# Attentional factorization machine on one core: 31 product columns per batch row in place of 32, products of both batch groups made at once

## What is computed

```python
F, B, K, H, VOCAB = 32, 2048, 64, 64, 12500      # sizes of this case
V = emb_v[x]                                      # F x B x K, gathered rows
iu, ju = np.triu_indices(F, k=1)
VV = V[iu] * V[ju]                                # 496 pairs of different fields
hid = relu(einsum('pbk,kh->pbh', VV, at_w) + at_b)
score = einsum('pbh,ho->pbo', hid, at_h)
pooled = sum(VV * score, axis=0)
logit = pooled @ p + w0 + sum(w1[x], axis=0)
y = sigmoid(logit)                                # B x 1
```

## Time and profile before

| | |
|---|---|
| runs | 842.78, 843.54 and 846.02 us, median 843.54 |
| span of the profiled execution | 835.8 us |
| median of the runs less that span | 7.7 us |
| mean TensorE clock granted | 0.992 of full |
| PE, DVE, ACT, POOL busy | 94%, 86%, 77%, 66% of the span |
| columns per PE matmul, rounds and scores | 512 |

### The profile page before, as it was taken

One profiled execution on the slowest core, in us unless ns is written; L12 is line 12 of the kernel. 1 busy time (PEld: TensorE's weight loads), 2 busy tenths in 40 slices (PEclk: granted clock), 3 DMA queues, 4 the chain that ended last, 5 costly groups with the idle time before them and its releaser, 6 DMA issues.

```text
span 835.8 us, 26345 instructions
## 1 busy us (share of the span) xinstructions
PE 784.1 (94%) x10550; PEld 277.6 (33%) x10550; DVE 722.5 (86%) x1221; ACT 640.7 (77%) x674; POOL 555.4 (66%) x537
## 2 busy tenths in 40 slices
PE   0488996999999999999999999999999999999998
PEld 0123332333333333333333333333333333333332
DVE  4278897699999999999999999999999999999894
ACT  0267775788798887878878788898888888888785
POOL 5577777666677676666766766677667666766720
PEclk9989998999999999999999999999999999999999
DMA  7533268445423466544332347644434457633200
GB/s 257 99 25 24 26 22 25 23 22 22 23 22 23 20 22 23 21 22 24 21 22 22 23 21 22 23 24 21 22 21 23 21 22 23 24 22 22 11 1 1
DMA packets 19398, 24.27 MB, mean 29 GB/s; under 512 B 9960, under 2 KB 10029, under 8 KB 19373
## 3 DMA queue, kind: packets, MB, share of 16 engines
q0 software_dynamic: 16896, 17.07, 43.4%
q1 hardware_dynamic: 1535, 6.64, 2.1%
q10 hardware_dynamic: 942, 0.22, 0.1%
HBM read 20.59 MB, written 3.31 MB: 29 GB/s over the span
## 4 chain that ended last, share of the span: by engine, by line
PE 86%; DMA 5%; POOL 5%; issue 2%; ACT 1%; DVE 0%; ACTq 0%; POOLq 0%
PE Z L591 52%; PE SG L607 26%; POOL rows L303 5%; PE SG L621 4%; PE Z L553 4%; DMA rows<-table,joint_idx 3%; DMA rows<-in_L_rec_emb_v_dram,idx 2%; ACT pV L471 0%; ACT H L526 0%; DMA idx_raw<-in_r_x_dram 0%; PE Z L685 0%; ACT V L460 0%; PE Z L664 0%; ACT y_sb L537 0%; ACTq L247 0%
## 5 line engine op out<-in xcount | busy, mean ns | idle before, releaser
L303 POOL DMA_INDIRECT rows<-table,joint_idx x496 | 518.8, 1046 | 224.0 <-issue 139.7
L445 DVE TENSOR_TENSOR X<-V 128x992 f32<-128x992 f32 (+15 forms) x1024 | 635.6, 692 | 28.8 <-ACT V L500 14.8
L526 ACT ACTIVATE H<-Z,bias 128x1024 f32<-128x1024 f32 x512 | 529.7, 1121 | 113.2 <-PE Z L591 109.8
L591 PE MATMUL Z<-X,w_sb 64*64 64x512 f32 x4096 | 477.2, 600 | 7.4 <-DVE X L445 3.4
L591 PEld LDWEIGHTS Z<-X,w_sb 64*64 64x64 f32 x4096 | 147.0, 132 | 288.7 <-issue 283.2
L607 PE MATMUL SG<-H,score_w 128*32 128x512 f32 x2048 | 239.4, 597 | 0.0
L607 PEld LDWEIGHTS SG<-H,score_w 128*32 128x32 f32 x2048 | 56.8, 109 | 172.8 <-issue 96.0
L471 ACT ACTIVATE pV<-V,pmask 128x1024 f32<-128x1024 f32 x64 | 81.5, 1276 | 0.1
L413 DVE TENSOR_TENSOR prod<-SG,gram 128x512 f32<-128x512 f32 x32 | 22.1, 691 | 63.3 <-PE SG L607 63.3
L460 ACT COPY V<-Z 128x1024 f32<-128x1024 f32 x31 | 31.4, 1013 | 42.4 <-PE Z L553 42.4
L621 PEld LDWEIGHTS SG<-V,pV 128*32 128x32 f32 x4096 | 42.7, 109 | 23.9 <-issue 19.3
(11 more groups left out here) (46 smaller groups left out, 35.1 us busy)
## 6 DMA issues: line engine op xcount, KB each, us to landing
rows<-table,joint_idx POOLq DMA_INDIRECT x496, 3.7
table<-joined SPq DMA_DIRECT2D x4, 792.0 KB
H<-in_L_rec_emb_v_dram SPq DMA_DIRECT2D x4, 768.0 KB, 8.3
rows<-in_L_rec_emb_v_dram,idx POOLq DMA_INDIRECT x16, 5.3
w_all<-in_L_rec_w_dram,idx POOLq DMA_INDIRECT x16
idx_raw<-in_r_x_dram SPq DMA_DIRECT2D x2, 64.0 KB, 2.1
idx_raw<-in_r_x_dram ACTq DMA_DIRECT2D x2, 64.0 KB, 2.3
table<-tail SPq DMA_DIRECT2D x1, 54.7 KB
```

The lines of the kernel that those rows point to most:

```text
L303: pool.indirect_dma_start(out=rows[t % 2][:, g * FILL_M + m, half, c0:c1], out_offset=None, in_=source, in_offset=bass.IndirectOffsetOnAxi ...
L445: last_one = nc.vector.tensor_tensor(xo, vj, vi.unsqueeze(3).to_broadcast(shape), ALU.mult)
L526: nc.scalar.activation(H[:, s % H_SLOTS, :, COLS * g:COLS * g + COLS], Z[:, z_slot(t, r), :, :], ACT.Relu, bias=bias[:, 0:1]).then_inc(hid ...
L591: done = nc.tensor.matmul(Z[64 * par:64 * par + 64, z_slot(t, r), half, :], w_sb[k, :], X[k, s % X_SLOTS, par, COLS * g:COLS * g + COLS], ...
```

## The change

A step's product vectors get 31 columns (`PAIRS`) in place of 32, so a group's row of columns is 16 x 31 = 496 (`COLS`), and the PSUM tile `Z` keeps banks of 512 (`BANK`). The column at 2s, which held pairs of the second kind and could hold a field with itself, now holds two pairs of neighbours: V[2s] x V[2s+1] and V[16+2s] x V[17+2s]. They are made by a TENSOR_TENSOR of their own (`own`, `other`). The other columns are made by two instructions of even widths, 30 - 2s and 2s; the second falls away at s = 0.

DVE makes a whole step for both groups in one go (`multiply`), except in the first half of the first fill. So there are 3 DVE instructions a step (2 at s = 0) where there were 4. `x_ready` counts steps, and DVE waits before a step for both rounds of the step four earlier. PE's `hidden` waits for the step. `mask_gram`, `weigh` and `sum_pairs` work on 31 and 15 columns. The scores are written to 31 of each 32 words of `SG`. `H` shrinks with `COLS`, and the table rows that are staged in it at the start begin one slot earlier.

```diff
-COLS = GROUP * FIELDS
+PAIRS = FIELDS - 1
+COLS = GROUP * PAIRS
+BANK = GROUP * FIELDS
...
-RAW_SLOT = 5
+RAW_SLOT = 4
...
-    low = 2 * s + 1
-    return [(2 * s, low, FIELDS, 0), (HALF_FIELDS + 2 * s, 0, low, HALF_FIELDS)]
+    low = 2 * s
+    upper_fields = (low, low + 1, PAIRS, 1)
+    last_fields = (HALF_FIELDS + low, 0, low, HALF_FIELDS)
+    return [upper_fields] + [last_fields] * (s > 0)
...
+            def multiply(parity, s, b0, b1):
+
+                xs = X[:, s % X_SLOTS, :, b0 * PAIRS:b1 * PAIRS].rearrange("p c (b j) -> p c b j", j=PAIRS)
+                fields = V[parity][:, b0:b1, :]
+                for i, c0, c1, shift in segments(s):
+                    shape = [128, 2, b1 - b0, c1 - c0]
+                    vj = fields[:, :, shift + c0:shift + c1].unsqueeze(1).to_broadcast(shape)
+                    vi = fields[:, :, i:i + 2].rearrange("p b c -> p c b")
+                    nc.vector.tensor_tensor(xs[:, :, :, c0:c1], vj, vi.unsqueeze(3).to_broadcast(shape), ALU.mult)
+                i, end = 2 * s, HALF_FIELDS + 2 * s + 1
+                own = fields[:, :, i:end + 1:HALF_FIELDS + 1].rearrange("p b c -> p c b")
+                other = fields[:, :, i + 1:end:HALF_FIELDS - 1].rearrange("p b c -> p c b")
+                nc.vector.tensor_tensor(xs[:, :, :, i], own, other, ALU.mult).then_inc(x_ready, 1)
...
-                    if not first:
-                        dve.wait_ge(z_ready, ROUNDS * t + r - 2 * X_SLOTS + 1)
-                    elif s >= X_SLOTS:
-                        dve.wait_ge(z_ready, FIRST_ORDER.index((s - X_SLOTS, g)) + 1)
...
+                    if first:
+                        dve.wait_ge(z_ready, FIRST_ORDER.index((s - X_SLOTS, 1)) + 1)
+                    else:
+                        dve.wait_ge(z_ready, ROUNDS * t + 2 * (s - X_SLOTS + 1))
+                    multiply(parity, s, 0, 2 * GROUP)
...
-                    nc.scalar.activation(H[:, s % H_SLOTS, :, COLS * g:COLS * g + COLS], Z[:, z_slot(t, r), :, :], ACT.Relu,
+                    nc.scalar.activation(H[:, s % H_SLOTS, :, COLS * g:COLS * g + COLS], Z[:, z_slot(t, r), :, 0:COLS], ACT.Relu,
...
-                        done = nc.tensor.matmul(Z[64 * par:64 * par + 64, z_slot(t, r), half, :], w_sb[k, :],
+                        done = nc.tensor.matmul(Z[64 * par:64 * par + 64, z_slot(t, r), half, 0:COLS], w_sb[k, :],
...
-                        last = nc.tensor.matmul(SG[parity][at:at + 32, :, :], score_w[:, s, :],
-                                                hid.rearrange("p (b j) -> p b j", j=FIELDS),
+                        last = nc.tensor.matmul(SG[parity][at:at + 32, :, 0:PAIRS], score_w[:, s, :],
+                                                hid.rearrange("p (b j) -> p b j", j=PAIRS),
```

More of the change, by code:

```diff
@@ L422, in products, with first_products @@
+            def first_products():
+                for r in range(STEPS):
+                    s, g = FIRST_ORDER[r]
+                    if r in (0, STEPS // 2):
+                        dve.wait_ge(first_v, g + 1)
+                    multiply(0, s, g * GROUP, (g + 1) * GROUP)
             def products(t, parity, first, last):
-                if not first:
+                if first:
+                    first_products()
+                else:
                     dve.wait_ge(v_ready, t)
-                for r, (s, g) in enumerate(FIRST_ORDER if first else ORDER):
-                    if first and r in (0, STEPS // 2):
-                        dve.wait_ge(first_v, g + 1)
-                    if r == 8:
+                for s in range(STEPS // 2 if first else 0, STEPS):
+                    if s == 4:
@@ L578, in hidden @@
             def hidden(t, r, first, last):
-                pe.wait_ge(x_ready, ROUNDS * t + r + 1)
+                s, g = (FIRST_ORDER if first else ORDER)[r]
+                if not first:
+                    pe.wait_ge(x_ready, multiplied(t) + s + 1)
+                else:
+                    pe.wait_ge(x_ready, r + 1 if r < STEPS else STEPS + s - STEPS // 2 + 1)
                 if r == turn_before(t) + 2 and not first and not last:
@@ L586, in hidden @@
                 pe.nop(nofuse=True)
-                s, g = (FIRST_ORDER if first else ORDER)[r]
                 for half in range(2):
```

43 lines of the change are left out of this document (19 added, 24 removed).

## The result

The changed kernel takes 970.19 us (median of 4 runs, 965.21 to 972.47) beside 843.16 for the kernel before (4 runs, 839.35 to 846.02): 1.151 times as long, 95% interval 1.1475 to 1.155. The forecast was 826.6. PE's columns went as forecast where PE ran unbroken, and what made the time was an instruction of GpSimd that the forecast had costed at nothing.

The account below looks back on a forecast made before the run. PE was taken as the bound, 24.12 us a fill, with savings from 136.01 us on. Columns save 18.4 us, ACT's pace takes back 1.5: span 835.8 - 16.9 = 818.9, plus 7.7 gives 826.6 us; range 821.5 to 832.5.

Parts of the forecast that it names:

- PE's columns: PE's matmuls after 136.01 us: 16 columns fewer save 26.7 ns a round or step of scores, 18.4 us in all.
- ACT's pace: ReLUs between PE's rounds: their pace limits six-round stretches, taking back 1.5 us of PE's gain.
- Rival (b): ACT's ReLU on two rows of 496 doesn't get shorter: 4.6 us less gain, 831.2 us; 5%.
- DVE stays hidden: DVE's work in a fill falls from 22.28 to 21.2 us, its wait growing to 2.3; slack, worth no time.
- Rival (a): DVE becomes the bound because rows of 31 words cost more; 832 us at 1.20 ns an element; 2%.
- the odd-word rule: DVE rows starting on odd words lose full rate: 4.0 us more a fill, about 873 us if true everywhere.
- (c): PE's scores: the gap in SG costs a column each, so scores gain nothing; 6.2 us less gain, 832.8; 5%.
- (d): PE's scores: every run of 31 in the output costs a short matmul's edge; 104 us, 930 in all; 4%.
- Whole steps in place of rounds: DVE making both groups before a step's first round: no new loop wait, at most 1 us in the first fill, covered.
- (f): PE's matmul sets are paced by issue and not by columns: 843.5 us; 2%.
- (e): POOL's gathered rows of fill 4 land earlier, PE's turn coming at about 132: 822.5 us; 7%.
- The term of 7.7 us: Added to the forecast span of 818.9 us as what the median has over the span.

Follow-up runs that it names:

- e12: Bench with no part of the model: ten stages of 16 gathers, each beside one kind of DVE stream; a gather took 0.94 us in the quiet stage.
- e1: Changed kernel with each of its two wide product instructions split again by batch group; ratio 1.024 to the kernel before, which took 1140.5 us there.
- e16: Second bench: five stages of 20 gathers, each behind a GpSimd instruction of varying length, beside the kernels' DVE shapes; longest gather 62.6 us.
- e2: Kernel before, 32 columns, each product instruction made for both batch groups at once; ratio 0.901 where the kernel before took 1140.5 us.
- e3: Changed kernel without the strided 128x64 instruction, one product left out; ratio 0.901 where the kernel before took 1140.5 us.
- e8: Changed kernel without the strided 128x64 instruction, one product left out, run again; ratio 0.897 where the kernel before took 1140.1 us.
- e10: Changed kernel without the strided 128x64 instruction, one product left out, run again; ratio 0.903 where the kernel before took 1120.0 us.
- e11: Changed kernel with a contiguous, unread 128x64 instruction in place of the strided one, one product left out; ratio 0.908 where the kernel before took 1120.0 us.
- e17: Kernel before with product instructions joined over both batch groups, 32 columns, nothing strided; 948.3 us against 840.8 for the kernel before, ratio 1.128.
- gated ones: Changed kernel, and 31 columns with one instruction a vector, each with a 128x8 reduction per step added; 0.922 and 0.952 on one chip, the latter 1.045 on another.
- e5: Kernel before, unchanged, run again for its trace; ratio 1.012 to itself, which took 1140.1 us there.
- e6: Changed kernel, unaltered, run on another chip; ratio 0.951 where the kernel before took 1140.1 us.

## Why the prediction was wrong, point by point

**PE's columns: right.** Where PE runs unbroken, the chain that ended last in the changed kernel has the three numbers that were forecast as 5.35, 2.63 and 3.49:

```profile
401.51 5.39 PE Z L617 x48
406.90 2.63 PE SG L633 x24
409.53 3.49 PE Z L617 x32
```

By these a PE that ran through would have had its fill of 23.5 us. Groups by shape, 180 to 900 us (busy, mean ns | idle before), beside the earlier trace rows:

```profile
L549 ACT ACTIVATE H<-Z,bias 128x992 f32<-128x992 f32 x404 | 406.9, 1092 | 94.1 <-PE Z L617 94.0
L617 PE MATMUL Z<-X,w_sb 64*64 64x496 f32 x3240 | 379.6, 605 | 1.2
L633 PE MATMUL SG<-H,score_w 128*32 128x496 f32 x1600 | 181.9, 584 | 0.0
...
L443 DVE TENSOR_TENSOR X<-V 128x64 f32<-128x64 f32 x202 | 57.6, 285 | 0.0
L439 DVE TENSOR_TENSOR X<-V 128x1920 f32<-128x1920 f32 x25 | 54.4, 2175 | 0.0
...
L439 DVE TENSOR_TENSOR X<-V 128x128 f32<-128x128 f32 x25 | 7.6, 305 | 0.0
```

The matmuls of a round have a mean of 605 ns with 496 columns, against 598 with 512: over the whole stretch the lower clock took the gain and a little more.

**ACT's pace: right.** 1092 ns for a ReLU, 1094 forecast. Rival (b) falls.

**DVE stays hidden: right on size.** The strided instruction is 285 ns long, 250 forecast, and takes 0.20 us of DVE's time (461.35 to 461.55), 0.18 forecast. An element costs 1.04 ns in rows of 31 words, (2175 - 305) / 1792, as in rows of 32. Rival (a) has no support, and neither has the odd-word rule of the Trainium skill (Vector Engine (DVE) Microarchitecture Reference, 5.2 Measured stream behaviour on trn2) for these rows. DVE got its slack: it was busy 695.3 us in place of 722.5, 0.85 us less for each of 32 fills where 1.1 was forecast.

**Rivals (c) and (d): neither.** 2.63 us for three steps of scores leaves no room for a column or an edge per run of 31. (f) falls by the same number, since scores got shorter with their columns, and (e) by the turn of fill 4, which came later and not earlier.

**Whole steps in place of rounds: the step that failed.** It looked for harm in three places, all between DVE and PE, and found none; PE indeed waits for DVE only in the first fills. In the first fill the wait grew from 1.14 to 2.74 us, by 1.6 where 1.1 was forecast. The failure is its last sentence: gathers "come a little earlier with PE; the queue is POOL's own in either kernel". The issue of the queue is POOL's own; the instruction is not, since it can be held by what DVE does. The description ahead of the forecast has the engines meet "only through semaphores"; the long gather at 460.14 and the product beside it have none between them, and the gather stood still for 13 us. The term that was left at 0 measured 16 x 0.397 = 6.4 us a fill in POOL's time. 2.6 us of that were slack; the other 3.8 are 106 us over 28 fills, and the turn of fill 4, which the earlier trace rows has at 136.01, comes at 151.99. That is 122 of the 127.6 us. (The turns give 4.2 us a fill, 113 us from fill 4 to the last.)

**What stood in the rows.** The trace of before had it, in numbers that the forecast never asked for. POOL's gathers had a median of 947 ns and a mean of 1046, up to 1978: 105 of 496 over 1 us. The gather in the earlier trace rows took 0.95. And POOL was busy 66%, with 0.30 us behind each gather that isn't counted as busy, so its true load was 16 x 1.35 of 24.1 us, 89%. A rival "gathers get longer" would have had a price at once: with PE's fill at 23.5 us, 23.5 / 16 - 1.35 = 0.12 us on each gather is all that POOL can lose before it is the bound.

**Range and chances.** The rival on the slower side was priced on PE's edges and not on the engine whose load per fill was nearest behind PE's and DVE's. 75% of the chances stood on the forecast and 93% on faster; the gain that they rested on was there wherever PE ran unbroken, and no chance at all stood on longer gathers. The term of 7.7 us was misread too: the changed kernel's profiled run took 965.21 us for a span of 963.4, so some 1.8 us lie around a span, and the span of 835.8 belongs, by that estimate, to an execution of about 838 us, quicker than all four that were timed. The forecast doesn't hang on it, since it is the median less 16.9.

## What to carry over

Count an engine's load in a loop with the gaps that always follow its instructions, not with its busy share: 66% was 89%. When an edit lengthens or joins VectorE instructions, look at every GpSimd instruction that runs beside them, and at the spread of its durations in the trace before: a mean above the median there is a hold that the edit can change. If VectorE must run long unbroken series of two-SBUF-input products, short instructions of another kind between them bound the hold, but they don't shorten the usual one.

## What the runs showed of the hardware

- A gather by indirect DMA is a GpSimd instruction of 0.94 us that is held by VectorE products with both inputs in SBUF (1.83 to 2.01 us in five stages of the bench e12) and by SBUF copies (1.90). It is not held by products with an input in PSUM (0.94), nor when it starts beside a reduction (29 of them in the changed kernel, none over 0.95).
- The two holds differ (e12): beside products a held gather ends 0.82 us after the end of a VectorE instruction, beside copies 0.12 us after it.
- A gather that is held by products gets in at the first boundary of two VectorE instructions after its start, and is then done 0.82 us later; or it misses that boundary and stays out until the series breaks off, up to 15.6 us in the kernels (e1) and 62.6 us in the bench (e16). What decides whether it misses stayed open. It happened with and without the strided instruction; at most three times in each of e2, e3, e8, e10, e11 and e17 (two instructions a step, or the contiguous third), and 18 to 29 times in each of the kernels with the strided one or with one instruction a vector, gated ones left out. The rule of the Trainium skill (SBUF — State Buffer, Who interferes with whom) has the ports held for one instruction, which describes the first kind alone.
- The same kernel took 841 and 843 us on two chips and 1120 to 1143 on four others, where 145 us of PE's idle time are put down to "issue" (e5) against 2, and the changed kernel was 15% slower on one chip of the first kind and 5% faster on one of the second (e6). What holds PE there was not tried.
